# A graph network's two convolution passes: 52 and 52 groups of edges for the two ways of reading, in place of 48 and 56

## The chip, the cores and the metric

The kernel runs on one core of one Trainium2 chip. The metric is the device time of one execution in microseconds (us), with all inputs in HBM at its start and the output there at its end.

## What is computed

The graph has 3125 nodes with 32 features each and 100000 edges, sorted by destination. Four blocks follow each other, each added to its input and normalized by row. Only the second and the third matter here:

```
# block 0: an edge network of four dense layers, averaged per destination (not touched)
# block 1
norm = deg_inv_sqrt[row] * deg_inv_sqrt[col]
x = layernorm(x + segment_sum(x[row] * norm[:, None], col, num_segments=n))
# block 2
h = x * rsqrt(max(deg_out, 1))[:, None]
agg = segment_sum(h[src], dst, num_segments=n) * rsqrt(max(deg_in, 1))[:, None]
x = layernorm(x + relu(agg @ weight + bias))
# block 3: three layers of graph attention (not touched)
```

Both blocks are a convolution of one form: for every edge read one row of a table of 3125 x 32 numbers at the edge's source, and add it up at the edge's destination.

## The kernel before

**The edges.** The sorted edges lie in 832 slots of 128 edges, 8 slots to a group, so 104 groups (`G`). The node numbers are split into 25 windows of 128 nodes (`W`). A slot's destinations lie in one window.

**The table** is written once per pass, to DRAM (`table`, `store_table`, L560) and to SBUF (`tab`). In SBUF each row is also kept as three bf16 parts whose sum is the float32 number (`tabparts`).

**Two ways to handle a group.** The 104 groups are split into two lists, the same in both passes (L55, L56).
- A *plain* group is gathered: GpSimd issues eight indirect DMAs (L396), each of which brings the 128 table rows of one slot into one of four buffers (`rows4`). VectorE makes the one-hot matrix of the destinations for the group's eight slots (L1658). TensorE multiplies (`sum_plain`, L935 to L945, eight matmuls, 128 x 96 each), and VectorE adds four results into the accumulator `acc` (L1617), at windows that it reads from a register load (`found`, L1607).
- A *dense* group is read on TensorE. A stationary matrix `bt` (128 x 1024 for each of four residues, bf16) says which source each edge has modulo 512; a matmul with all of the table picks seven candidates for each edge (`read`, L905 to L920, 24 matmuls for two slots). VectorE masks them by the group of 512 that the source lies in (`gmask`, L1630, and L1638) and reduces them to one (L1645). TensorE then multiplies by the float32 one-hot of the destinations, which SP loads from DRAM (`dhot`, L558), in `sum_dense` (L922 to L933), and VectorE adds the result into `acc` (L1617). This is done in four items of two slots each.

**Who makes `bt`.** In pass 1 it is VectorE, a quarter at each item, one group ahead (`stationary`, L1620, the comparison at L1633). In pass 2 it is ScalarE (`act_stationary`, L736 to L744).

**The order.** `ITEMS` (L59) is a fixed order that TensorE and VectorE both walk: all 192 dense items, with the 56 plain groups spread evenly among them, so three or four dense items lie between two plain groups. TensorE does `read(i)` and then `sum_dense(i - 1)`. Two PSUM banks take the reads and two the sums, so `read(i)` waits for the mask of item i - 2 and `sum_dense(i - 1)` for the reduction of item i - 1. A plain sum waits for its one-hot and for its gathered rows (L937, L938).

**The degrees.** In pass 1 the out-degrees of the nodes are counted as well, in 104 steps spread over the order: ScalarE makes the one-hot (L730, L733), VectorE the other factor (L1670), TensorE does eight small matmuls (`degree`, L947 to L953).

**GpSimd** issues the gathers in order (`pool_convolution`, L380). It waits for the plain sum that frees a buffer (L391) and stays at most `LEAD` = 24 gathers ahead of TensorE's dense reads (L395). **SP** loads for each dense group the numbers of which `bt` is made (`numbers_of`, L538) and the hot matrix, two groups ahead (`sp_convolution`, L548).

Of the kernel before, what the change touches and what calls it, by code (L numbers as in the profile page):

```python
# [27 lines left out]
C = 32  # L28
# [25 lines left out]
GROUPS = -(-W // FOLD)  # L54
DENSE = [g for g in range(G) if 6 * g % 13 >= 7]  # L55
PLAIN = [g for g in range(G) if 6 * g % 13 < 7]  # L56
LEAD = 24
ND, NP, NS = len(DENSE), len(PLAIN), 4 * len(DENSE)
ITEMS = [x for i in range(NS) for x in [("dense", i)] + [("plain", p) for p in range(NP * i // NS, NP * (i + 1) // NS)]]  # L59
BIG = 1e30  # L60
# [14 lines left out]
def build(nc, x, edge_blocks, L0, W_gcn, b_gcn, gat, out):  # L75
    with ExitStack() as ctx:
# [303 lines left out]
        def pool_convolution(pool, pas):  # L380

            if pas == 1:
                pool.wait_ge(small_turned, 1)
            else:
                pool.wait_ge(x_given, 2)
            pool.memset(acc[:, :, 0:3 * C], 0.0).then_inc(acc_zeroed, 1)
            pool.wait_ge(table_stored, 16 * (pas + 1))
            for p_, g in enumerate(PLAIN):
                at = (pas - 1) * NP + p_
                if at >= 4:  # L390
                    pool.wait_ge(plain_summed, at - 3)  # L391
# [142 lines left out]
        def stationary_there(d):  # L534

            return (bt_made, FOLD * (d + 1)) if d < ND else (bt2_made, FOLD * (d - ND + 1))

        def numbers_of(sp, pas, d):  # L538

            at, g = (pas - 1) * ND + d, DENSE[d]  # L540
            if at == 0:
# [6 lines left out]
        def sp_convolution(sp, pas):  # L548

            sp.wait_ge(table_stored, 16 * (pas + 1))  # L550
            for d, g in enumerate(DENSE):
                at = (pas - 1) * ND + d
# [183 lines left out]
        def act_stationary(act, d):  # L736

            b, at = d % 2, d - ND
            act.wait_ge(r_in[b], 16 * (d // 2 + 1))
# [24 lines left out]
        def _(act):  # L764
# [136 lines left out]
        def pe_convolution(pe, pas):  # L901

            base, dbase = (pas - 1) * NP, (pas - 1) * ND

# [55 lines left out]
            counted = 0  # L960
            for n, (kind, i) in enumerate(ITEMS):
                if kind == "dense":
# [3 lines left out]
                else:  # L966
                    sum_plain(i)
                while pas == 1 and counted < G and counted * len(ITEMS) < (n + 1) * G:
                    degree(counted)
                    counted += 1  # L970
            sum_dense(NS - 1)
            if pas == 1:
# [276 lines left out]
        def _(v):  # L1249
# [352 lines left out]
            def gcn(pas):  # L1602

                base, dbase = (pas - 1) * NP, (pas - 1) * ND
                order = [(acc_zeroed, pas)]
# [14 lines left out]
                def stationary(d, k):  # L1620
                    if d >= dbase + ND:
                        return
                    b = d % 2
                    if k == 0:
                        v.wait_ge(r_in[b], 16 * (d // 2 + 1))
                        if d >= 2:
                            v.wait_ge(dense_read, 4 * (d - 1))
                            v.wait_ge(picked_made, 4 * (d - 1))
                        g = DENSE[d - dbase]
                        link(v.tensor_tensor(gmask[:, b, :, :], wide(grp[:, 8 * g:8 * g + 8], GROUPS),  # L1630
# [23 lines left out]
                def plain_one_hot(p_):  # L1654
                    if p_ >= NP:
                        return
                    at, g = base + p_, PLAIN[p_]
                    v.tensor_tensor(hotb[:, at % 2, :, :], wide(dloc[:, 8 * g:8 * g + 8], P), down(ps[:, IOTA, 0:P], 8),  # L1658
# [23 lines left out]
                def run():  # L1682
                    counted = 2
                    for n, (kind, i) in enumerate(ITEMS):
                        if kind == "dense":
                            stationary(dbase + i // 4 + 1, i % 4)
                            pick(i)
                            if i % 4 == 0:
                                places[i // 4 % 2] = found(DENSE[i // 4], C)
                            if i > 0:  # L1690
                                add_dense(i - 1)
                        else:
                            plain_one_hot(i + 1)
                            add_plain(i, found(PLAIN[i], 3 * C))
                        while pas == 1 and counted < G and (counted - 2) * len(ITEMS) < (n + 1) * G:
                            degree_groups(counted)
                            counted += 1
                    add_dense(NS - 1)
                    v.wait_ge(*order[0])
# [347 lines left out]
```

## Time and profile before

| | us |
|---|---|
| median of three runs | 5590.19 |
| lowest and highest of them | 5585.79, 5603.41 |
| the profiled execution | 5609.76 |
| its span | 5608.0 |

Of the span, some 605 us belong to pass 1 of the convolutions (first dense read at 1039.6 us to the last reduction at 1644.4) and 574 us to pass 2 (1664.0 to 2237.6); block 0 is ahead of them and the attention behind. The profile gives for each engine its busy time and its timeline. "issue" as the cause of a wait means that the engine waited for nothing that the profile shows. On GpSimd the time between two gathers is partly work of its own that isn't booked as busy. L943 is a plain sum, L916 a dense read, L931 a dense sum, L951 a degree step; of a float32 sum two matmuls are listed as four.

### The profile page before, as it was taken

What the parts mean: (1) busy time and instruction counts of PE and PEld (TensorE: products, weight loads), DVE (VectorE), ACT (ScalarE), POOL (GpSimd) and SP (SyncE); (2) the same over time, 40 slices, a digit from 0 to 9 for tenths busy, and PEclk for the clock granted to TensorE, in tenths of its full rate; (3) what the DMA queues carried; (4) which work ended last, traced back from release to release, by engine and by line L of the source; (5) the groups of instructions that cost most, each with busy time, mean ns of one, the idle gap of its engine ahead of it and who ended that gap; (6) DMA issues with size and microseconds to landing.
All of it is one profiled execution on the core that took longest, in us unless ns stands there. A gap on an engine that the chain in (4) does not pass through costs nothing.

```text
span 5608.0 us, 137304 instructions
## 1 busy us (share of the span) xinstructions
PE 4951.9 (88%) x47173; PEld 3418.4 (61%) x47173; DVE 3662.6 (65%) x7001; ACT 2121.6 (38%) x3942; POOL 3829.5 (68%) x3980
## 2 busy tenths in 40 slices
PE   4999999789879998599999986999999769999997
PEld 3777777688878888255555552555555535555555
DVE  7566555699987777465666674666666746666667
ACT  2222222466656665233333323333333233333331
POOL 5777777477747776677777716777777177777770
PEclk9999999799989999799999997999999889999998
DMA  5755555233323333344444423444444234444442
GB/s 141 190 169 164 170 164 168 71 96 102 96 78 102 102 102 86 82 128 126 130 127 127 128 71 85 129 128 130 128 126 127 64 95 125 129 130 127 127 126 60
DMA packets 694505, 667.15 MB, mean 119 GB/s; under 512 B 398707, under 2 KB 485242, under 8 KB 693818
## 3 DMA queue, kind: packets, MB, share of 16 engines
q1 hardware_dynamic: 558442, 489.21, 28.8%
q0 software_dynamic: 127424, 164.72, 13.7%
q10 hardware_dynamic: 7952, 4.46, 0.5%
q8 instruction: 383, 6.28, 0.5%
q14 instruction: 304, 2.49, 0.1%
HBM read 568.30 MB, written 89.59 MB: 117 GB/s over the span
## 4 chain that ended last, share of the span: by engine, by line
PE 41%; POOL 26%; issue 19%; DVE 6%; DMA 5%; ACT 2%; DVEq 1%; SPq 0%; POOLq 0%; ACTq 0%
POOL rows L376 16%; PE ps L916 11%; PE ps L1071 10%; POOL rows L363 10%; PE ps L1010 5%; DMA rows<-table,idx 3%; PE ps L1031 3%; PE ps L931 2%; PE ps L1045 2%; PE ps L996 1%; DVE region L1638 1%; ACT region L683 1%; PE ps L1021 1%; DVE acc L1617 1%; PE ps L880 1%
## 5 line engine op out<-in xcount | busy, mean ns | idle before, releaser
L376 POOL DMA_INDIRECT rows<-table,idx x2340 | 2263.2, 967 | 990.5 <-issue 681.6
L1071 PE MATMUL ps<-region,hot 128*128 128x272 f32 x4992 | 1296.2, 404 | 61.8 <-issue 33.5
L683 ACT ACTIVATE region<-ps 128x512 f32<-128x512 f32 x1248 | 678.0, 596 | 1579.1 <-PE ps L1010 1579.1
L1805 DVE TENSOR_TENSOR acc<-acc,ps 128x272 f32 x1248 | 544.9, 437 | 921.2 <-PE ps L1071 812.3
L1071 PEld LDWEIGHTS ps<-region,hot 128*128 128x128 f32 x4992 | 905.1, 191 | 347.0 <-issue 173.2
L916 PE MATMUL ps<-hot,region 128*128 128x192 bf16 (+1 forms) x9216 | 875.4, 253 | 37.8 <-DVEq L1308 20.6
L363 POOL DMA_INDIRECT rows<-table,idx x728 | 703.9, 967 | 243.5 <-issue 220.5
L916 PEld LDWEIGHTS ps<-hot,region 128*128 128x128 bf16 x9216 | 810.4, 101 | 44.9 <-DVEq L1308 20.7
L1780 DVE TENSOR_TENSOR region<-ps,region 128x1056 f32<-128x1056 f32 x582 | 724.9, 1252 | 45.3 <-issue 40.3
L1010 PE MATMUL ps<-xT,wcat 64*128 64x512 f32 x2496 | 710.3, 646 | 9.5 <-ACT region L683 9.2
L396 POOL DMA_INDIRECT rows<-table,idx x448 | 426.6, 952 | 172.2 <-issue 120.2
L396 POOL DMA_INDIRECT region<-table,idx x448 | 426.6, 952 | 137.1 <-issue 119.2
L996 PEld LDWEIGHTS ps<-identb,rows 128*32 128x32 bf16 x7020 | 221.7, 99 | 426.8 <-issue 426.8
L996 PE MATMUL ps<-identb,rows 128*32 128x128 bf16 x7020 | 274.0, 225 | 185.2 <-DMA rows<-table,idx 184.7
L1010 PEld LDWEIGHTS ps<-xT,wcat 64*128 64x128 f32 x2496 | 190.1, 186 | 359.9 <-issue 358.3
L1645 DVE TENSOR_REDUCE region<-region 128x64 f32<-128x448 f32 x384 | 358.1, 933 | 13.2
L730 ACT ACTIVATE region<-iota,region 128x128 bf16<-128x128 f32 x832 | 254.3, 389 | 218.0 <-PE ps L951 215.0
L1031 PE MATMUL ps<-region,attblk 128*32 128x512 f32 x2496 | 315.0, 624 | 0.0
L1638 DVE TENSOR_TENSOR region<-ps,gmask 128x448 f32<-128x448 f32 x384 | 238.0, 620 | 100.3 <-PE ps L916 97.5
L931 PE MATMUL ps<-region 128*128 128x32 f32 x1536 | 220.4, 267 | 67.9 <-issue 59.7
L1497 DVE TENSOR_TENSOR acc<-acc,ps 128x65 f32 x416 | 93.3, 224 | 284.0 <-PE ps L880 180.5
L742 ACT ACTIVATE region<-region,lanes 128x1024 bf16<-128x1024 f16 x192 | 204.8, 1137 | 191.0 <-PE ps L916 191.0
(302 smaller groups left out, 6723.5 us busy)
## 6 DMA issues: line engine op xcount, KB each, us to landing
hot<-hot_dram SPq DMA_DIRECT2D x624, 256.0 KB
turned<-turned_dram SPq DMA_DIRECT2D x624, 128.0 KB
rows<-table,idx POOLq DMA_INDIRECT x3516
hot_dram<-hot SPq DMA_DIRECT2D x104, 512.0 KB
region<-hot_dram SPq DMA_DIRECT2D x96, 512.0 KB
xwin<-table SPq DMA_DIRECT2D x1664, 24.0 KB
region<-r_dram SPq DMA_DIRECT2D x109, 256.0 KB, 5.9
region<-d_dram SPq DMA_DIRECT2D x104, 256.0 KB
```

The lines of the kernel that those rows point to most:

```text
L363: pool.indirect_dma_start(rows[:, g % 3, j, :], None, table, bass.IndirectOffsetOnAxis(ap=idx[:, 8 * g + j:8 * g + j + 1], axis=0)).then_i ...
L376: pool.indirect_dma_start(rows[:, n % 2, j, :], None, table, bass.IndirectOffsetOnAxis(ap=idx[:, s:s + 1], axis=0)).then_inc(rows_in3[n % ...
L396: pool.indirect_dma_start(rows4[at % 4][:, j, :], None, table, bass.IndirectOffsetOnAxis(ap=idx[:, 8 * g + j:8 * g + j + 1], axis=0)).then ...
L683: act.activation(rz[g % 2][:, 2 * t + side, :], ps[:, Z + side, :], ACT.Relu).then_inc(rz_made, 1)
L916: mm = pe.matmul(ps[:, GB + i % 2, 224 * j:224 * j + n], bt[b][:, k, at:at + P], tabparts[:, k::FOLD, (2 + s) * C:(3 + s) * C], start=(k = ...
L996: mm = pe.matmul(ps[q:q + C, XT, j * P:(j + 1) * P], rowparts[(l * G + g) % 2][:, at, 2 * C + s * C:2 * C + (s + 1) * C], identb[:, :], st ...
L1010: pe.matmul(ps[:, Z + side, :], wcat[l][q:q + 64, side, t * P:(t + 1) * P], xT[q:q + 64, g % 2, :], start=True, stop=True).then_inc(z_summ ...
L1031: pe.matmul(ps[at:at + 32, LG, :], attblk[l][:, t, (3 - m) * H:(7 - m) * H], rz[g % 2][:, 2 * t + side, :], start=False, stop=(m == 3 and ...
L1071: mm = pe.matmul(ps[:, sum_bank(k, side, i), 0:PC + H], hot[:, b, 4 * side + 2 * i + j, :], px[b][:, 4 * side + 2 * i + j, :], start=(j == ...
L1645: v.tensor_reduce(found32[:, d % 2, at:at + 2, :], picked[d % 2][:, at:at + 2, :, :].rearrange("p j g c -> p j c g"), AX.X, ALU.add).then_ ...
L1780: v.tensor_tensor(to, at.unsqueeze(3).broadcast_to([P, 4, H, HK]), xs[:, (k // 8) % 2, k % 8, 4 * side:4 * side + 4, :].unsqueeze(2).broad ...
L1805: v.tensor_tensor(at, at, ps[:, sum_bank(k, side, i), 0:PC + H], ALU.add).then_inc(att_added, 1)
```

## The change

The two lists become every odd group (dense) and every even group (plain), 52 and 52, in both passes. The lists, the counts and the order become dictionaries by pass, with offsets (`FIRST_DENSE`, `FIRST_PLAIN`) in place of multiples of the old counts. The new order is: four dense items, one plain group, 52 times. `LEAD` stays at 24. The diff, cut to its core:

```diff
-DENSE = [g for g in range(G) if 6 * g % 13 >= 7]
-PLAIN = [g for g in range(G) if 6 * g % 13 < 7]
+DENSE = {1: [g for g in range(G) if g % 2 == 1], 2: [g for g in range(G) if g % 2 == 1]}
+PLAIN = {pas: [g for g in range(G) if g not in DENSE[pas]] for pas in (1, 2)}
 LEAD = 24
-ND, NP, NS = len(DENSE), len(PLAIN), 4 * len(DENSE)
-ITEMS = [x for i in range(NS) for x in [("dense", i)] + [("plain", p) for p in range(NP * i // NS, NP * (i + 1) // NS)]]
+ND, NP = ({pas: len(of[pas]) for pas in (1, 2)} for of in (DENSE, PLAIN))
+NS = {pas: 4 * ND[pas] for pas in (1, 2)}
+FIRST_DENSE, FIRST_PLAIN = {1: 0, 2: ND[1]}, {1: 0, 2: NP[1]}
+ITEMS = {pas: [x for i in range(NS[pas]) for x in [("dense", i)] + [("plain", p) for p in range(
+    NP[pas] * i // NS[pas], NP[pas] * (i + 1) // NS[pas])]] for pas in (1, 2)}
...
-            for p_, g in enumerate(PLAIN):
-                at = (pas - 1) * NP + p_
+            for p_, g in enumerate(PLAIN[pas]):
+                at = FIRST_PLAIN[pas] + p_
...
-                    read = (8 * p_ + j - LEAD) * NS // (8 * NP)
+                    read = (8 * p_ + j - LEAD) * NS[pas] // (8 * NP[pas])
                     if read > 0:
-                        pool.wait_ge(dense_read, (pas - 1) * NS + read)
+                        pool.wait_ge(dense_read, 4 * FIRST_DENSE[pas] + read)
...
-            for d in range(ND, ND + 2):
+            for d in range(ND[1], ND[1] + 2):
                 act_stationary(act, d)
...
-            for d in range(ND + 2, 2 * ND):
+            for d in range(ND[1] + 2, ND[1] + ND[2]):
                 act_stationary(act, d)
...
-            base, dbase = (pas - 1) * NP, (pas - 1) * ND
+            base, dbase = FIRST_PLAIN[pas], FIRST_DENSE[pas]
...
-            for n, (kind, i) in enumerate(ITEMS):
+            for n, (kind, i) in enumerate(ITEMS[pas]):
```

The rest of it replaces the same names in the same way, on SP, TensorE, ScalarE and VectorE.

## Rows read from the trace of the kernel before

**Rows 1.** Passes 1 and 2: length, busy PE, PEld, DVE, ACT, POOL; clock; DMA.
```profile
1056.91:1640.93 584.02, 522.25 (x6521) 508.43 (x6522) 528.46 (x1169) 366.60 (x907) 420.73 (x439) 0.99 0.34 95
1682.64:2234.11 551.47, 502.04 (x5707) 490.72 (x5707) 430.03 (x886) 366.79 (x230) 414.67 (x439) 0.98 0.35 100
```

**Rows 2.** TensorE's timeline: last plain sum of pass 1, both ends of pass 2.
```profile
1640.93 0.50 PE L943 MATMUL ps<-region 128*128 128x96 bf16 x8
...
1682.64 0.50 PE L943 MATMUL ps<-rows,region 128*128 128x96 bf16 x8
...
2234.11 0.51 PE L943 MATMUL ps<-region 128*128 128x96 bf16 x8
```

**Rows 3.** GpSimd's timeline: last gather of pass 1, first and last of pass 2.
```profile
1610.70 0.95 POOL L396 DMA_INDIRECT region<-table,idx  x1 [0.31 <-PE ps L916]
...
1670.66 0.95 POOL L396 DMA_INDIRECT rows<-table,idx  x1 [8.77 <-DMA table<-hot]
...
2229.95 0.95 POOL L396 DMA_INDIRECT region<-table,idx  x1 [0.30 <-issue]
```

**Rows 4.** TensorE's waits ahead of plain sums, pass 2: us in total, times, longest.
```profile
PE ps L943 <- issue: 21.4, 21, 2.3
...
PE ps L943 <- DVE region L1658: 10.8, 4, 3.0
```

**Rows 5.** VectorE's groups of instructions, pass 1: busy, mean ns, idle before.
```profile
L1645 DVE TENSOR_REDUCE region<-region 128x64 f32<-128x448 f32 x188 | 175.2, 932 | 6.4
...
L1638 DVE TENSOR_TENSOR region<-ps,gmask 128x448 f32<-128x448 f32 x188 | 116.0, 617 | 11.6 <-PE ps L916 11.0
...
L1633 DVE TENSOR_SCALAR region<-region,lanes 128x1024 bf16<-128x1024 f16 x184 | 92.8, 504 | 1.6
...
L1658 DVE TENSOR_TENSOR region<-dloc,ps 128x1024 bf16<-128x1024 f32 x55 | 66.8, 1214 | 0.2 <-issue 0.2
```

**Rows 6.** TensorE's timeline, pass 1, between two plain sums.
```profile
1270.49 0.50 PE L943 MATMUL ps<-rows,region 128*128 128x96 bf16 x8
1270.84 2.22 PE L916 MATMUL ps<-hot,region 128*128 128x224 bf16 x24
...
1273.29 0.35 PE L951 MATMUL ps<-region 128*128 128x25 bf16 x8
...
1282.42 0.50 PE L943 MATMUL ps<-rows,region 128*128 128x96 bf16 x8
```

**Rows 7.** VectorE's timeline, pass 1: one-hots beside the two plain sums of rows 6.
```profile
1271.92 1.21 DVE L1658 TENSOR_TENSOR region<-dloc,ps 128x1024 bf16<-128x1024 f32 x1
...
1283.84 1.21 DVE L1658 TENSOR_TENSOR region<-dloc,ps 128x1024 bf16<-128x1024 f32 x1
```

**Rows 8.** Busy time by engine over seven stretches from plain sum to plain sum.
```profile
1270.49:1282.42 11.93, 10.97 (x138) 10.58 (x138) 10.97 (x25) 7.22 (x19) 8.96 (x10) 1.00 0.35 100
1492.91:1505.06 12.15, 10.97 (x138) 10.58 (x138) 11.08 (x25) 7.21 (x19) 9.39 (x10) 1.00 0.36 100
1568.11:1579.91 11.80, 10.98 (x139) 10.58 (x139) 10.72 (x25) 5.88 (x17) 8.97 (x10) 1.00 0.34 101
1345.32:1356.87 11.55, 11.31 (x137) 10.94 (x138) 10.62 (x25) 6.00 (x18) 8.81 (x10) 0.96 0.35 101
2023.29:2034.16 10.87, 10.37 (x123) 10.17 (x123) 8.82 (x19) 7.98 (x6) 8.22 (x9) 1.00 0.37 108
2162.68:2173.29 10.61, 10.31 (x120) 10.23 (x121) 8.53 (x18) 7.68 (x6) 8.17 (x9) 1.00 0.41 110
1741.98:1752.13 10.15, 10.15 (x120) 10.15 (x121) 7.12 (x16) 6.19 (x5) 7.71 (x9) 1.00 0.38 111
```

**Rows 9.** TensorE's timeline, pass 1: a waiting dense sum, the read behind it.
```profile
1191.76 0.60 PE L931 MATMUL ps<-region 128*128 128x32 f32 x4 [1.67 <-issue]
...
1192.41 3.88 PE L916 MATMUL ps<-hot,region 128*128 128x224 bf16 x24
```

**Rows 10.** GpSimd's gathers of both passes into one buffer pair, min/median/max ns.
```profile
L396 POOL DMA_INDIRECT region<-table,idx x448: 941/947/1196, 1065.7 to 2230.0; - x150
```

More of the change, by code:

```diff
@@ L534, in stationary_there @@
         def stationary_there(d):
-            return (bt_made, FOLD * (d + 1)) if d < ND else (bt2_made, FOLD * (d - ND + 1))
+            return (bt_made, FOLD * (d + 1)) if d < ND[1] else (bt2_made, FOLD * (d - ND[1] + 1))
         def numbers_of(sp, pas, d):
-            at, g = (pas - 1) * ND + d, DENSE[d]
+            at, g = FIRST_DENSE[pas] + d, DENSE[pas][d]
             if at == 0:
@@ L550, in sp_convolution @@
             sp.wait_ge(table_stored, 16 * (pas + 1))
-            for d, g in enumerate(DENSE):
-                at = (pas - 1) * ND + d
+            for d, g in enumerate(DENSE[pas]):
+                at = FIRST_DENSE[pas] + d
                 b = at % 2
@@ L736, in act_stationary @@
         def act_stationary(act, d):
-            b, at = d % 2, d - ND
+            b, at = d % 2, d - ND[1]
             act.wait_ge(r_in[b], 16 * (d // 2 + 1))
@@ L967, in pe_convolution @@
                     sum_plain(i)
-                while pas == 1 and counted < G and counted * len(ITEMS) < (n + 1) * G:
+                while pas == 1 and counted < G and counted * len(ITEMS[pas]) < (n + 1) * G:
                     degree(counted)
                     counted += 1
-            sum_dense(NS - 1)
+            sum_dense(NS[pas] - 1)
             if pas == 1:
@@ L1602, in gcn @@
             def gcn(pas):
-                base, dbase = (pas - 1) * NP, (pas - 1) * ND
+                base, dbase = FIRST_PLAIN[pas], FIRST_DENSE[pas]
                 order = [(acc_zeroed, pas)]
@@ L1620, in stationary @@
                 def stationary(d, k):
-                    if d >= dbase + ND:
+                    if d >= dbase + ND[pas]:
                         return
@@ L1628, in stationary @@
                             v.wait_ge(picked_made, 4 * (d - 1))
-                        g = DENSE[d - dbase]
+                        g = DENSE[pas][d - dbase]
                         link(v.tensor_tensor(gmask[:, b, :, :], wide(grp[:, 8 * g:8 * g + 8], GROUPS),
@@ L1654, in plain_one_hot @@
                 def plain_one_hot(p_):
-                    if p_ >= NP:
+                    if p_ >= NP[pas]:
                         return
-                    at, g = base + p_, PLAIN[p_]
+                    at, g = base + p_, PLAIN[pas][p_]
                     v.tensor_tensor(hotb[:, at % 2, :, :], wide(dloc[:, 8 * g:8 * g + 8], P), down(ps[:, IOTA, 0:P], 8),
@@ L1683, in run @@
                     counted = 2
-                    for n, (kind, i) in enumerate(ITEMS):
+                    for n, (kind, i) in enumerate(ITEMS[pas]):
                         if kind == "dense":
@@ L1688, in run @@
                             if i % 4 == 0:
-                                places[i // 4 % 2] = found(DENSE[i // 4], C)
+                                places[i // 4 % 2] = found(DENSE[pas][i // 4], C)
                             if i > 0:
@@ L1693, in run @@
                             plain_one_hot(i + 1)
-                            add_plain(i, found(PLAIN[i], 3 * C))
-                        while pas == 1 and counted < G and (counted - 2) * len(ITEMS) < (n + 1) * G:
+                            add_plain(i, found(PLAIN[pas][i], 3 * C))
+                        while pas == 1 and counted < G and (counted - 2) * len(ITEMS[pas]) < (n + 1) * G:
                             degree_groups(counted)
                             counted += 1
-                    add_dense(NS - 1)
+                    add_dense(NS[pas] - 1)
                     v.wait_ge(*order[0])
```

## The prediction

> **What bounds the kernel now.** I cut the profile by stage first: only the two convolution passes run differently after the change, so the question is which engine sets the pace in each. A table of busy times over the stretch from the first to the last plain sum of a pass [rows 1] shows three engines nearly full in both: TensorE 522 of 584 us and 502 of 551 us, VectorE 528 and 430 us. GpSimd's 421 and 415 us look like slack, but its timeline corrects that: the 448 gathers of pass 2 start from 1670.66 to 2229.95 us [rows 3], one every 559.29 / 447 = 1.251 us, of which only 0.95 is booked as busy. In pass 2 GpSimd never rests.
>
> So the passes differ. In **pass 1** the last gather starts at 1610.70 us [rows 3] and the last plain sum at 1640.93 us [rows 2]: the gathers are 30 us ahead, and TensorE and VectorE set the end. VectorE has the more work there [rows 1]. In **pass 2** the last gather starts 4.2 us before the last plain sum [rows 2, 3]. The waits name the cost: TensorE waits 21.4 + 10.8 = 32.2 us ahead of plain sums [rows 4]. The longer waits are put down to a one-hot, yet that matrix is made one plain group earlier; what these sums lack is the last gathered row of the group, and I book all 32.2 us as waits for gathers.
>
> **What the change removes and adds, in each pass.** Four plain groups go, four dense ones come, and the order becomes regular: four dense items, one plain group, 52 times over.
> - GpSimd: 32 gathers fewer, 32 x 1.251 = 40.0 us.
> - TensorE: a dense item (24 reads and the sum after it) takes 1273.29 - 1270.84 = 2.45 us, a plain group 1270.84 - 1270.49 = 0.35 us [rows 6]. Together 16 x 2.45 - 4 x 0.35 = +37.8 us.
> - VectorE: 16 times mask and reduction, 0.617 + 0.932, and in pass 1 a quarter of a stationary, 0.504; four one-hots of 1.214 fewer [rows 5]. The additions into the accumulator stay, 16 for 16. That is +28.0 us in pass 1 and +19.9 in pass 2.
> - ScalarE makes the stationaries of pass 2 itself. It is busy 7.98 us in a cycle of 10.87 [rows 8], so a group's matrix is ready before its turn: nothing.
> - SP: four loads of the hot matrix and four of the numbers more per pass. They keep their place, two groups ahead, and run beside gathers that are fewer: nothing. Were a load late, TensorE would stand for as long as it is late, every cycle.
>
> These sums can't simply be taken, since the engines hand items to each other through two PSUM banks. But the new order already stands in the trace. Wherever a plain group ends on a group border and four dense items follow before the next one, the old kernel runs exactly one new cycle; that happens seven times in each pass. So I measure cycles.
>
> **Pass 1.** The cycle from 1270.49 to 1282.42 us takes 11.93 us [rows 6, 8]. TensorE is busy 10.97 and VectorE 10.97 of it [rows 8]; VectorE's rest is mostly a register load at each dense group's start. Does it repeat itself? VectorE starts the one-hot beside the plain sum 1271.92 - 1270.49 = 1.43 us behind TensorE at its start and 1283.84 - 1282.42 = 1.42 at its end [rows 6, 7]: the lag is handed on unchanged, so this is the steady cycle. It also has two degree steps, what each new cycle gets. The seven run from 11.55 to 12.15 us [rows 8], three of them within 0.02 of this one. So 51 x 11.93 = 608.4 us stands against 584.02 [rows 1], **+24.4 us**. The two additions from above agree in kind: VectorE's 28.0, less some of its waits for TensorE of 11.0 us [rows 5].
>
> **Pass 2.** Here the seven are mixed up with gather waits: where TensorE stood before a plain sum, VectorE caught up, and the cycle after it is short, 10.15 us [rows 8], TensorE's bare work (4 x 2.45 + 0.35). Undisturbed it is 10.87 us [rows 8]; three of the seven are within 0.02 of that. The 0.7 us above bare work is TensorE waiting for the first reduction after a plain group: one-hot, four additions and the mask come before it on VectorE. In the new kernel nothing lets VectorE catch up, so 10.87 is the price. A group's gathers take 8 x 1.251 = 10.0 us, less than the cycle, so once ahead they stay ahead. 51 x 10.87 = 554.4 against 551.47 us [rows 1], **+2.9 us**: the 32.2 us of gather waits go, and so does the half-clock work behind them, but 37.8 us of matmuls and a wait for VectorE in every cycle take their place.
>
> Start and tail of each pass keep their order: nothing. **Sum:** 24.4 + 2.9 = +27.3. The profiled execution took 5609.76 us, so its own forecast is 5637. That execution lies 0.35% above the median of the three runs, 5590.19; the difference carries over: 5590.2 + 27.3 = 5617.5, say 5617 us.
>
> **A rule weighed.** A gather is booked with 0.947 us at the median and 1.196 at most, beside all the vector work of both passes [rows 10]. The Trainium skill (SBUF — State Buffer, on the three doors into it) says that while VectorE runs a copy-like instruction in its two-port mode, GpSimd can't write descriptors and the gather waits it out. By it every new comparison would stop the gathers for its length. This trace disagrees on the size.
>
> **The rivals.**
> - *Short cycles hold.* If VectorE's lag settles lower, the cycles are 11.80 and 10.61 us, both seen [rows 8]: 51 x 11.80 - 584.02 = +17.8 and 51 x 10.61 - 551.47 = -10.4, together +7.4, 5598 us. For it: most pass-2 cycles of the kind are under 10.87. Against: each of those follows a wait that goes away. 15%.
> - *Faster: the gathers were the real bound.* The place is the first reduction behind each plain group. If VectorE arrives there in time, as after the old gather waits, pass 2 runs at 10.15, 51 x 10.15 = 517.7, -33.8 us, and pass 1 at its shortest, 11.55 [rows 8], 589.1, +5.0: -28.8, 5561 us. It decides once the two cycles together are below (584.02 + 551.47) / 51 = 22.26 us, where mine are 22.80. Against it: the steady lag of rows 6 and 7, and that the 11.55 had TensorE slow at its start (granted 0.96 [rows 8]). 4%.
> - *The clock.* After a wait of 1.67 us TensorE's next read took 3.88 us in place of 2.2, at the lower of its levels, 1.2 GHz [rows 9]. My cycles are all at 2.4 GHz. If the waits of 0.7 us also bring such drops, they cost about what they cost now, by the granted clock of 0.99 and 0.98 [rows 1]: 0.01 x 584 + 0.02 x 551 = +17, 5634 us. A pass-1 cycle of 12.15 throughout would give as much (+11). 8%.
> - *The gathers become the bound of pass 1.* If each of the four comparisons of a cycle stops GpSimd for its 0.504 us, a group's gathers take 10.0 + 2.0 = 12.0 us, over the 11.93 of the cycle: 51 x 12.0 = 612, +4 on the sum, 5621 us; this is what the rule above makes of it. But the same comparisons run now at gathers 1.251 us apart. 1%.
>
> That the change does not do what it says is excluded by the diff: the lists and their counts give 52 and 52.
>
> **How the numbers follow.** A measurement can tell about 0.3%, 17 us, from no change. The forecast, with 72%, is slower by more; so are the clock and gather rivals, 9% together. The short cycles are within 0.3%, and the faster case is beyond it: slower 0.81, same 0.15, faster 0.04. The range runs from the short cycles, 5598, to the clock's end, 5634; it leaves out the faster case and the outer half of noise.
>
> **What would show it.** Right: plain sums 11.9 us apart in pass 1 and 10.9 in pass 2, to within 0.1; no wait ahead of plain sums in pass 2 after its first cycles; TensorE waiting ahead of the dense sums instead (the line of the 0.7 us), once or twice a cycle; GpSimd's gathers no longer 1.251 us apart throughout but held back by reads; 32 gathers fewer per pass, and everything outside the passes unchanged. Wrong: a pass-2 cycle near 10.15 would say that VectorE catches up by itself; half-clock reads inside the cycles would say that waits of 0.7 us cost clock; a wait for the hot matrix would say that SP's loads are late.

## The result and the profile after

The changed kernel takes **5627.26 us** at the median of five runs (5617.68 to 5638.17), the kernel before 5590.32 us (5585.79 to 5603.41) in five runs beside it. The ratio is **1.0049** with a 95% interval from 1.0033 to 1.0066: slower, by 18 to 37 us. The two medians lie 36.9 us apart, at the upper end of that interval. The profiled execution took 5632.79 us with a span of 5631.0; the one before took 5609.76.

In the code after, everything behind the new lists stands three lines lower: a plain sum is L946, a dense read L919, a dense sum L934, a degree step L954, the addition L1620, the comparison L1636, mask and reduction L1641 and L1648, the one-hot L1661, a gather L399.

First the passes, cut again from the first to the last plain sum (length, busy PE, PEld, DVE, ACT, POOL; clock; DMA), which answers to [rows 1]:

```profile
1060.72:1673.48 612.76, 559.76 (x6939) 539.60 (x6939) 557.01 (x1218) 369.77 (x907) 397.44 (x407) 1.00 0.36 94
1713.89:2267.81 553.92, 528.50 (x6120) 518.44 (x6121) 448.40 (x917) 397.76 (x250) 383.91 (x407) 1.00 0.39 103
```

Pass 1 went from 584.02 to 612.76 us, **+28.7**, pass 2 from 551.47 to 553.92, **+2.5**: +31.2 together. The reader is to see the columns too. VectorE has 28.6 and 18.4 us more work, TensorE 37.5 in pass 1 but only 26.5 in pass 2, where 37.8 were added: most of the missing 11 us are old reads that no longer run at the lower clock (granted 0.98 before, 1.00 now). The 4512 matmuls of the old reads were booked with 427.4 us, the 4896 of the new ones with 453.7; at the new mean the old ones would have taken 9 us less. GpSimd has the 32 gathers fewer.

The span grew by 23.0 only, since the stretches outside the passes together took 8.2 us less: +3.8 ahead of the first plain sum, -1.3 between the passes, -10.7 behind them. Nothing is changed there, and they scatter: in the profiles below, the first plain sum comes between 1043 and 1067 us, and the rest behind pass 2 takes 3361 to 3376 us. So I read every kernel below by its two passes and use the ratios as the check. Where the same pass is profiled again its length repeats to within 3 us: 582.22 to 584.77 for the old pass 1, 553.91 to 555.22 for the new pass 2.

TensorE's waits over the two passes (time in total, times, longest), which answer to [rows 4]; the first row is pass 1, the others are pass 2:

```profile
PE ps L934 <- issue: 52.9, 100, 0.9
...
PE ps L934 <- issue: 25.4, 50, 0.8
PE ps L946 <- issue: 0.7, 1, 0.7
```

The 32.2 us ahead of plain sums in pass 2 have become 0.7. In their place TensorE waits 50 times for 0.5 us ahead of a dense sum (30 times, 16.9 us, before). Such a wait costs 0.7 us: from the read's start to the sum's start it takes 2056.12 - 2053.39 = 2.73 us in place of 2.06, since a sum that needn't wait starts ahead of the booked end of the read. TensorE's and VectorE's timelines over one cycle of pass 2 show the place:

```profile
2050.60 0.50 PE L946 MATMUL ps<-region 128*128 128x96 bf16 x8
2050.94 2.22 PE L919 MATMUL ps<-hot,region 128*128 128x224 bf16 x24
2053.00 0.56 PE L934 MATMUL ps<-region 128*128 128x32 f32 x4
2053.39 2.22 PE L919 MATMUL ps<-hot,region 128*128 128x224 bf16 x24
2056.12 0.60 PE L934 MATMUL ps<-region 128*128 128x32 f32 x4 [0.50 <-issue]
...
2061.46 0.50 PE L946 MATMUL ps<-rows,region 128*128 128x96 bf16 x8
```

```profile
2052.02 1.21 DVE L1661 TENSOR_TENSOR region<-dloc,ps 128x1024 bf16<-128x1024 f32 x1
2053.15 1.11 DVE L1620 TENSOR_TENSOR acc<-acc,ps 128x96 f32 x4
2054.18 0.21 DVE L1633 TENSOR_TENSOR gmask<-region,iota 128x56 f32<-128x56 f32 x1
2054.43 0.62 DVE L1641 TENSOR_TENSOR region<-ps,gmask 128x448 f32<-128x448 f32 x1
2055.08 0.93 DVE L1648 TENSOR_REDUCE region<-region 128x64 f32<-128x448 f32 x1
```

The cycle is 2061.46 - 2050.60 = 10.86 us. The dense sum at 2056.12 needs the reduction that ends at 2056.01; ahead of that VectorE does the one-hot, four additions, the group mask and the mask, in one row without a gap. The one-hot starts 2052.02 - 2050.60 = 1.42 us behind the plain sum, as in [rows 6, 7].

GpSimd's last gather of pass 1 and the first and last of pass 2, which answer to [rows 3]:

```profile
1637.09 0.94 POOL L399 DMA_INDIRECT region<-table,idx  x1 [0.30 <-issue]
...
1702.53 0.95 POOL L399 DMA_INDIRECT rows<-table,idx  x1 [8.07 <-DMA table<-hot]
...
2234.15 0.95 POOL L399 DMA_INDIRECT region<-table,idx  x1 [0.30 <-issue]
```

The gathers end 2267.81 - 2234.15 = 33.7 us ahead of the last plain sum of pass 2, where they were 4.2 ahead. No wait for them is left in this pass but the 0.7 us.

### The profile page after: what moved, and what is told of

Same layout as the page of the kernel before. It is cut to its first block, busy times and chain, and to the rows that moved or that the text cites. A ratio compares the mean times of both kernels' runs of the same rounds, so it can differ in the third digit from the quotient of the medians.

```text
span 5631.0 us, 139144 instructions
## 1 busy us (share of the span) xinstructions
PE 5010.4 (89%) x48005; PEld 3478.4 (62%) x48005; DVE 3712.7 (66%) x7081; ACT 2153.3 (38%) x3962; POOL 3767.1 (67%) x3916
## 4 chain that ended last, share of the span: by engine, by line
PE 46%; POOL 27%; issue 17%; DMA 4%; DVE 3%; ACT 2%; DVEq 0%; SPq 0%; POOLq 0%; ACTq 0%
POOL rows L379 15%; PE ps L919 15%; POOL rows L366 11%; PE ps L1074 11%; PE ps L1013 5%; PE ps L934 3%; PE ps L1034 3%; DMA rows<-table,idx 3%; PE ps L1048 2%; PE ps L999 1%; PE ps L1024 1%; ACT region L686 1%; PE ps L946 1%; PE ps L993 1%; PE ps L874 0%
## 5 line engine op out<-in xcount | busy, mean ns | idle before, releaser
L379 POOL DMA_INDIRECT rows<-table,idx x2340 | 2254.4, 963 | 1019.5 <-issue 687.0
L919 PE MATMUL ps<-hot,region 128*128 128x192 bf16 (+1 forms) x9984 | 932.9, 250 | 20.7 <-DVEq L1311 20.7
L919 PEld LDWEIGHTS ps<-hot,region 128*128 128x128 bf16 x9984 | 865.5, 100 | 22.4 <-DVEq L1311 20.8
L366 POOL DMA_INDIRECT rows<-table,idx x728 | 704.0, 967 | 246.4 <-issue 221.0
L399 POOL DMA_INDIRECT rows<-table,idx x416 | 399.8, 961 | 195.8 <-issue 104.8
L399 POOL DMA_INDIRECT region<-table,idx x416 | 399.7, 961 | 162.3 <-issue 102.4
L1648 DVE TENSOR_REDUCE region<-region 128x64 f32<-128x448 f32 x416 | 388.1, 933 | 14.2
L1641 DVE TENSOR_TENSOR region<-ps,gmask 128x448 f32<-128x448 f32 x416 | 258.1, 621 | 90.6 <-PE ps L919 87.5
L934 PE MATMUL ps<-region 128*128 128x32 f32 x1664 | 240.1, 268 | 85.9 <-issue 80.3
L934 PEld LDWEIGHTS ps<-region 128*128 128x128 f32 x1664 | 219.2, 192 | 116.9 <-issue 110.8
L745 ACT ACTIVATE region<-region,lanes 128x1024 bf16<-128x1024 f16 x208 | 221.9, 1137 | 159.0 <-PE ps L919 159.0
```

The lines of the kernel that those rows point to most:

```text
L366: pool.indirect_dma_start(rows[:, g % 3, j, :], None, table, bass.IndirectOffsetOnAxis(ap=idx[:, 8 * g + j:8 * g + j + 1], axis=0)).then_i ...
L379: pool.indirect_dma_start(rows[:, n % 2, j, :], None, table, bass.IndirectOffsetOnAxis(ap=idx[:, s:s + 1], axis=0)).then_inc(rows_in3[n % ...
L399: pool.indirect_dma_start(rows4[at % 4][:, j, :], None, table, bass.IndirectOffsetOnAxis(ap=idx[:, 8 * g + j:8 * g + j + 1], axis=0)).then ...
L919: mm = pe.matmul(ps[:, GB + i % 2, 224 * j:224 * j + n], bt[b][:, k, at:at + P], tabparts[:, k::FOLD, (2 + s) * C:(3 + s) * C], start=(k = ...
L934: mm = pe.matmul(ps[:, DB[i % 2], 0:C], dhot[b][:, at, :], found32[:, b, at, :], start=(j == 0), stop=(j == 1))
```

## The experiments

What had to be told apart. The first theory (L where a text below uses a letter) is the prediction's: the length of a cycle is set by the chain behind each plain group on VectorE, with the lag that it hands on. Its rivals: VectorE's total of work sets it, whatever the order; the gathers still have a part; and, for the 4.3 us by which pass 1 missed its forecast, gathers that meet a comparison of VectorE (the collision theory, P). The kernel before was run again beside them; its median was 5602.68 us for the first four, 5602.57 for the next four, 5594.05 for the last three. "52" in the table is the new split of a pass, "48" the old; lengths are from first to last plain sum in us.

| run | split, passes 1 and 2 | pass 1 | pass 2 | ratio to before, 95% |
|---|---|---|---|---|
| before | 48, 48 | 584.02 | 551.47 | |
| after | 52, 52 | 612.76 | 553.92 | 1.0049 (1.0033 to 1.0066) |
| e1 | 48, 52 | 584.77 | 555.22 | 1.0006 (0.9991 to 1.0022) |
| e2 | 52, 48 | 611.83 | 550.43 | 1.0041 (1.0024 to 1.0059) |
| e3 one-hot later | 52, 52 | 626.42 | 530.60 | 1.0057 (1.0036 to 1.0078) |
| e4 plain group mid-way | 52, 52 | 601.50 | 542.66 | 1.0027 (1.0014 to 1.0040) |
| e5 one-hot in the first item | 52, 52 | 607.83 | 545.71 | 1.0022 (1.0008 to 1.0036) |
| e6 as e5, pass 2 only | 48, 52 | 582.22 | 545.20 | 0.9981 (0.9971 to 0.9991) |
| e7 LEAD 20 | 52, 52 | 608.16 | 553.98 | one run, 5621.06 us |
| e8 short comparisons | 52, 52 | 584.73 | 553.91 | one run, 5600.12 us |
| e9 one-hot and windows ahead | 52, 52 | 601.53 | 519.87 | 0.9980 (0.9969 to 0.9991) |
| e10 as e9 | 48, 52 | 577.62 | 518.93 | **0.9927** (0.9911 to 0.9944) |
| e11 as e9 | 48, 48 | 578.45 | 550.33 | 0.9990 (0.9978 to 1.0002) |

**The change in one pass alone.**

```diff
-DENSE = {1: [g for g in range(G) if g % 2 == 1], 2: [g for g in range(G) if g % 2 == 1]}
+DENSE = {1: [g for g in range(G) if 6 * g % 13 >= 7], 2: [g for g in range(G) if g % 2 == 1]}
```

> The new split in pass 2 alone; pass 1 keeps 48 and 56 groups. Nothing is left out of the computation. Theory L (the lag theory: VectorE's work behind each plain group, one-hot, four additions, mask, arrives late at the first reduction, so the repeating cycle of four dense items and one plain group costs 12.0 us in pass 1 and 10.87 us in pass 2): pass 1 takes 584 us from first to last plain sum as in the kernel before, pass 2 takes 554 us; +2 to +4 us against the kernel before, about 5593 us. Rival M (the loss is spread over both passes alike, each dense group costs about the same extra in either): half of the +37 us, about 5609 us. Rival S (the short cycles: pass 2 gains once the gather waits go): 10 to 30 us below the kernel before.

e2 has the two lists the other way round.

> The new split in pass 1 alone; pass 2 keeps 48 and 56 groups. Nothing is left out. Theory L: pass 1 takes 613 us from first to last plain sum as in the changed kernel, pass 2 551 us as before; +27 to +31 us against the kernel before, about 5619 us. Rival M: +18 us, about 5609 us. Rival S: as much above the changed kernel as pass 2 gained there.

The loss is pass 1's: 1.0041 with the change in pass 1 alone, 1.0006 with it in pass 2 alone; together 1.0047, against 1.0049 for both. Each pass is as long as in the full change to within 1.3 us (611.83 against 612.76, 555.22 against 553.92), so the passes hardly act on each other.

**The one-hot moved behind the second dense item.** If the chain sets the cycle, pass 2 should fall to TensorE's bare work.

```diff
+                    since, due = -9, 0
...
                             if i > 0:
                                 add_dense(i - 1)
+                            since += 1
+                            if since == 2:
+                                plain_one_hot(due)
                         else:
-                            plain_one_hot(i + 1)
+                            since, due = 0, i + 1
                             add_plain(i, found(PLAIN[pas][i], 3 * C))
```

> The changed kernel, 52 and 52, with VectorE's one-hot for the next plain group made behind the second dense item after a plain group and not beside the plain sum. VectorE does the same instructions. Theory L: the 1.1 us of the one-hot leaves the stretch ahead of the first reduction, TensorE no longer waits there in pass 2, and the cycle there falls from 10.87 to 10.15 to 10.25 us (TensorE's bare work), so pass 2 takes 518 to 523 us and not 554; in pass 1 VectorE is nearly full whatever its order, so the cycle falls only by part of VectorE's wait for TensorE of 0.2 us, to 11.6 to 11.9 us from 12.0: 6 to 20 us. Together 37 to 55 us below the changed kernel. Rival B (the 0.7 us per cycle are TensorE's own, a cost of changing between the kinds of items or of PSUM): both cycles stay, no difference from the changed kernel. Rival T (VectorE's total work sets both passes, not its order): no difference either.

Pass 2 fell by 23.3 us to cycles of 10.38; the 31 to 36 us and the 10.15 to 10.25 of the expectation were not reached. Pass 1 rose by 13.7, to cycles of mostly 12.2 to 12.4: a miss for the chain theory, which had it at 11.6 to 11.9. VectorE's timeline of e3 in pass 1 names what I had not counted:

```profile
1475.93 0.18 DVE L1620 TENSOR_TENSOR acc<-acc,ps 128x32 f32 x1
1476.66 1.12 DVE L1620 TENSOR_TENSOR acc<-acc,ps 128x96 f32 x4 [0.56 <-DVE acc L1620]
1477.70 0.21 DVE L1633 TENSOR_TENSOR gmask<-region,iota 128x56 f32<-128x56 f32 x1
```

Ahead of the four additions VectorE stands 0.56 us. The one-hot used to be issued between; while it ran for 1.21 us, the register load of the windows of those additions passed unseen. The waits of VectorE over pass 1 of e3 say that this happens in every cycle, and that VectorE waits for TensorE only 0.2 + 3.8 us in all 626:

```profile
DVE acc L1620 <- DVE acc L1620: 30.5, 53, 1.0
DVE acc L1620 <- issue: 26.5, 47, 0.6
DVE acc L1620 <- PE ps L934: 3.8, 4, 0.9
DVE region L1641 <- PE ps L919: 0.2, 1, 0.2
```

So in e3 VectorE is full in pass 1, by its two exposed register loads. One edit had taken a piece off the chain and put 0.56 us on the total.

**The plain group in the middle of a dense group.** The chain keeps its one-hot and its hidden register load, but the group mask, made at a dense group's start, leaves it.

```diff
-    NP[pas] * i // NS[pas], NP[pas] * (i + 1) // NS[pas])]] for pas in (1, 2)}
+    NP[pas] * (i + 2) // NS[pas], NP[pas] * (i + 3) // NS[pas]) if p < NP[pas]]] for pas in (1, 2)}
```

> The changed kernel, 52 and 52, with each plain group two dense items earlier: it stands in the middle of a dense group and no longer on the border between two, where VectorE also makes the mask (0.21 us) and reads a register for the windows (0.56 us without work). Theory L: only the mask leaves the stretch ahead of the reduction behind the plain group; the register load comes after that reduction anyway. TensorE's wait in pass 2 falls from 0.7 to about 0.45 us, the cycle from 10.87 to 10.6 us, pass 2 by 12 to 14 us; in pass 1 the cycle stays within 0.2 of 12.0. Together 5 to 20 us below the changed kernel. Rival C (the coincidence with the dense group's border is what costs, register load included): pass 2 falls to 10.2 us per cycle, 35 us. Rival B: nothing changes.

Most cycles fell to 11.72 to 11.75 and 10.60, by 0.2 to 0.3 us; the group mask is booked with 0.21 and takes 0.25 from its start to the next (2054.18 to 2054.43). The same instructions in another order, and both passes are shorter by 11.3 us: order counts, not the sum alone. In pass 1 about half of that probably belongs to another effect, lengthened comparisons (below), of which e4 has few: their mean is 488 ns in place of 517, over some 200 of them. VectorE now waits for reads 3.8 us in all of pass 1, so there it is full, at 11.73 us. Some 7 us were given back ahead of each pass's first plain sum, outside the lengths in the table: it waits 6.9 and 7.3 us, since it now comes before its gathered rows.

**The one-hot in the first dense item, ahead of the register load.**

```diff
                             pick(i)
+                            if due is not None:
+                                plain_one_hot(due)
+                                due = None
                             if i % 4 == 0:
...
-                            plain_one_hot(i + 1)
+                            if True:
+                                due = i + 1
+                            else:
+                                plain_one_hot(i + 1)
```

> The changed kernel, 52 and 52, with the one-hot for the next plain group made in the first dense item after the plain group, between that item's reduction and its register load. The run with the one-hot behind the second item showed that beside the plain sum it had hidden a register load of 0.57 us, which then stood bare. Here it hides the same load of the dense group, so VectorE's total stays as in the changed kernel. Theory L (what counts is how much of VectorE's work stands between a plain sum and the first reduction after it; there it is now 0.57 and not 1.13 us): TensorE's wait in pass 2 falls from 0.7 to 0.1 us, the cycle from 10.87 to 10.25 us, pass 2 to 523 to 526 us; pass 1, where VectorE is full, 11.6 to 11.9 us per cycle, 592 to 607 us. Together 35 to 50 us below the changed kernel. Rival R (an exposed register load costs more than the one-hot that hid it): pass 2 at 10.4 us as with the one-hot behind the second item, pass 1 at 12.2 us. Rival B (the 0.7 us are TensorE's own): no change.

Pass 2's cycle is 10.67, not the 10.25 expected; pass 1's 11.89, at the upper end of what was expected. The additions ahead again wait 0.56 us for their windows, so most of what the one-hot's leaving gave is taken back. e6 does the same in pass 2 alone, with the old list in pass 1.

> A version that might beat both: pass 1 with the old 48 and 56 in the old order, pass 2 with 52 and 52 and the one-hot in the first dense item after the plain group. Nothing is left out. Theory L: pass 1 584 us as before, pass 2 523 to 526 us in place of 551; 25 to 28 us below the kernel before, about 0.5%. Rival R: pass 2 at 530 us, 20 us below the kernel before. Rival M (each dense group costs the same extra in either pass): above the kernel before.

This is the first version that beats the kernel before, by 0.19% and not by the 0.5% expected: pass 2 takes 545.20 us, where 523 to 526 were expected, for the same reason as in e5.

**The collision.** From its sixteenth cycle on, pass 1 of the changed kernel takes 12.05 to 12.08 us in most cycles, in place of the 11.90 to 11.93 before that. Comparisons (VectorE) and gathers (GpSimd) of the changed kernel, first in an early cycle, then in a late one:

```profile
1099.99 0.94 POOL L399 DMA_INDIRECT rows<-table,idx  x1 [0.30 <-issue]
1100.32 0.49 DVE L1636 TENSOR_SCALAR region<-region,lanes 128x1024 bf16<-128x1024 f16 x1
...
1255.30 0.94 POOL L399 DMA_INDIRECT rows<-table,idx  x1 [0.30 <-issue]
1255.86 0.64 DVE L1636 TENSOR_SCALAR region<-region,lanes 128x1024 bf16<-128x1024 f16 x1
...
1258.92 0.48 DVE L1636 TENSOR_SCALAR region<-region,lanes 128x1024 bf16<-128x1024 f16 x1
1259.05 1.17 POOL L399 DMA_INDIRECT rows<-table,idx  x1 [0.30 <-issue]
```

The comparison at 1255.86 is the one in the chain behind the plain group. It starts 0.56 us into a gather and takes 0.15 us more, and the cycle is 0.14 longer. At 1259.05 it is the gather that starts in a comparison and takes 0.23 us more. Not every overlap does this: the comparison at 1100.32 begins 0.33 us into its gather and is not lengthened. The timelines of pass 1, before and after, show where the limits lie. All 95 comparisons that begin 0.49 to 0.69 us into a gather are longer, 0.50 to 0.70 us, and they end 1.18 to 1.20 us behind the gather's start; of the 108 that begin up to 0.45 us into one, none takes more than 0.49. All 88 gathers that begin 0.09 to 0.28 us into a comparison are longer, at least 1.03 us, and they end 1.28 to 1.31 us behind the comparison's start.

The kernel before had such comparisons too, one of them within the cycle that the prediction measured:

```profile
1281.52 0.62 DVE L1633 TENSOR_SCALAR region<-region,lanes 128x1024 bf16<-128x1024 f16 x1
```

That cycle still took 11.93 us, since its comparison is the fourth, behind which VectorE has time: the read that its next mask needs ends at 1282.19, and the mask starts at 1282.23. In the late cycles of the new kernel it is the first that grows, in 31 of the 36 from the sixteenth on. Gathers that run freely drift past the comparisons. In the late cycles they are held back by TensorE, by its plain sums (46.8 us from 1240 on) and its reads (29.4), so they come at the same point of every cycle. To shift them without touching VectorE I set another lead:

```diff
-LEAD = 24
+LEAD = 20
```

> The changed kernel with gathers at most 20 and not 24 ahead of the dense reads. In the changed kernel the cycle of pass 1 is 11.92 us while the gathers still run freely and 12.06 from about the fifteenth cycle on, when they are held back in step with TensorE; from there each cycle has the comparison of its first dense item at 0.64 in place of 0.49 us, beside the end of a gather. Theory P (a gather and a comparison of VectorE delay each other, and held-back gathers meet the same comparison in every cycle): with the gathers at another point of the cycle the late cycles of pass 1 are no longer 12.06: 11.92 if they meet none, up to 12.3 if they meet two or more, and the change comes earlier, at about the eighth cycle; pass 2, without comparisons on VectorE, stays at 10.87. Rival D (the longer late cycles have another cause, such as the loads from DRAM): 11.92 and then 12.06 at the same cycles as in the changed kernel.

VectorE's comparisons over pass 1 (count, busy, mean ns, idle before), in the changed kernel and in e7:

```profile
L1636 DVE TENSOR_SCALAR region<-region,lanes 128x1024 bf16<-128x1024 f16 x200 | 103.5, 517 | 1.8
```

```profile
L1636 DVE TENSOR_SCALAR region<-region,lanes 128x1024 bf16<-128x1024 f16 x200 | 98.9, 494 | 1.8
```

With the mean back at 494 ns, most cycles are 11.90 to 11.93 to the end and pass 1 takes 608.16 us: 4.6 us less for 4.6 us of comparisons. No comparison of a first dense item is longer than 0.5 us in e7, and pass 2 stays at 553.98 us. Comparisons of the fourth item are still lengthened, to 0.53 us and more in 20 cycles, and cost nothing. The gathers are booked with 974 and 975 ns at the mean in e7 and 978 and 979 in the changed kernel; they are lengthened as often, and TensorE has no wait for one in that pass. The Trainium skill (SBUF — State Buffer, on the two sides of the SBUF) calls the port pair of VectorE and GpSimd an exclusive lock: whichever starts first keeps it for its whole instruction. That each delays the other agrees with the rows, if the comparison is of the kind that takes the pair; "for its whole instruction" does not. By it the comparison at 1255.86 would have stood until the gather's end at 1256.24, 0.38 us in place of 0.15, and the one at 1100.32 until 1100.93, where it did not stand at all.

**Less work for VectorE.** From its third dense group on, e8 compares only 128 of 1024 columns of each quarter of the stationary in pass 1. The rest of that matrix is left as it was, so that part of the computation is missing.

```diff
-                        v.tensor_scalar(bt[b][:, k, :], rline[b], lanes[:, k:k + 1], None, ALU.is_equal).then_inc(bt_made, 1)
+                        e = 4 * P if d < 2 else P // 2
+                        v.tensor_scalar(bt[b][:, k, 0:2 * e], rline[b][:, 0:2 * e], lanes[:, k:k + 1], None, ALU.is_equal).then_inc(bt_made, 1)
```

> The changed kernel with VectorE's comparisons of pass 1 cut from 1024 to 128 columns from the third dense group on, so the stationary matrices of pass 1 are wrong there: a part of the computation is left out, to see what VectorE's work is worth. 200 comparisons of 0.5 us become about 0.1 us each. Theory L (VectorE sets pass 1): the cycle falls from 12.0 by 1.2 to 1.5 us, to 10.5 to 10.8 us, where TensorE's bare work with two degree steps (10.55 us) takes over; pass 1 takes 540 to 552 us and not 613. Rival B (TensorE or its hand-over sets pass 1): the cycle stays within 0.3 of 12.0 us. Rival G (the gathers set it): the same.

The cycle fell to 11.46, by 0.45, and not to 10.5 to 10.8. VectorE's timeline of e8 (the comparison is L1637 there, the mask L1642), and then of the changed kernel:

```profile
1272.60 0.25 DVE L1637 TENSOR_SCALAR region<-region,lanes 128x128 bf16<-128x128 f16 x1
1272.76 0.62 DVE L1642 TENSOR_TENSOR region<-ps,gmask 128x448 f32<-128x448 f32 x1
```

```profile
1270.98 0.48 DVE L1636 TENSOR_SCALAR region<-region,lanes 128x1024 bf16<-128x1024 f16 x1
1271.37 0.62 DVE L1641 TENSOR_TENSOR region<-ps,gmask 128x448 f32<-128x448 f32 x1
```

From one start to the next a comparison went from 0.39 to 0.16 us, 0.23 less. Four of them take 0.92 us off VectorE's total. The cycle lost 0.45 (11.91 to 11.46), which is two of them. VectorE's waits for reads grew from 11.3 us to 34.7. So VectorE's total did not set this cycle, the chain did. That the chain crosses two comparisons on its way from the plain group to the waits of TensorE is my reading of the 0.45, not shown apart. The expectation, 10.5 to 10.8, took the whole of VectorE's savings off the cycle and was wrong.

**Both at once: the one-hot moved, and its windows loaded behind it.** The register load goes where e3 has the one-hot, so that it is hidden again, and the additions find their windows in registers. The edit against e3:

```diff
-                    counted = 2
-                    since, due = -9, 0
+                    counted, since, due, held = 2, -9, 0, found(PLAIN[pas][0], 3 * C)
...
                             since += 1
-                            if since == 2:
+                            if since == 2 and due < NP[pas]:
                                 plain_one_hot(due)
+                                held = found(PLAIN[pas][due], 3 * C)
                         else:
                             since, due = 0, i + 1
-                            add_plain(i, found(PLAIN[pas][i], 3 * C))
+                            add_plain(i, held)
```

> The changed kernel, 52 and 52, with the one-hot for the next plain group behind the second dense item (as in the run that moved it there) and the register load of that group's windows behind the one-hot, kept in registers until the plain group's turn. The load is then hidden again, and nothing but four additions and a mask stands between a plain sum and the first reduction. Theory L (the order of VectorE's work behind a plain group sets the cycle of both passes; the split alone does not): pass 2 10.15 to 10.25 us per cycle, 518 to 523 us; pass 1 11.3 to 11.7 us per cycle, 576 to 597 us; 45 to 70 us below the changed kernel, 15 to 35 below the kernel before. Rival T (VectorE's total work sets pass 1): pass 1 at 11.9 us per cycle, since the total is the changed kernel's, and only pass 2 gains. Rival R (loading and keeping the registers ahead costs as much): pass 2 at 10.4, pass 1 at 12.2.

Pass 2 runs at 10.15 us, TensorE's bare work: 519.87 us, of which TensorE is busy 519.87. Pass 1 runs at 11.77 to 11.80 in most cycles, above the 11.3 to 11.7 expected, so as a whole e9 is 10 us below the kernel before and not 15 to 35. VectorE's waits over pass 1 of e9:

```profile
DVE acc L1620 <- issue: 26.9, 48, 0.9
DVE acc L1620 <- PE ps L934: 2.7, 3, 0.9
DVE region L1641 <- PE ps L919: 0.5, 2, 0.4
```

VectorE waits for a read 0.5 us in the whole pass. It is full, as in e4: with one register load left open (0.56 in a cycle, the first row) its total is 11.7 to 11.8 us. The changed kernel's 11.92 stood 0.1 to 0.2 above that. To get pass 1 below, the load of the dense group's windows would have to be hidden as well, beside that of the plain group; no run tries both.

**The same order with each split.** e10 has the old list in pass 1 and the new one in pass 2; e11 the old one in both.

> The same move of one-hot and windows in both passes, with the old 48 and 56 in pass 1 and 52 and 52 in pass 2. Theory L: pass 2 518 to 523 us; pass 1, where gathers allow 56 x 10.0 = 561 us, 565 to 580 us in place of 584; 35 to 50 us below the kernel before. Theory T: pass 1 stays at 584 us, 28 to 33 us below the kernel before.

> The same move in both passes with the old 48 and 56 in both: what the move is worth without the new split. Theory L: in pass 2 the gathers set the time at 56 x 1.251 x 8 = 560 us from first gather to last, so pass 2 stays at 548 to 552 us from first to last plain sum, however little VectorE waits; pass 1 565 to 580 us; 5 to 20 us below the kernel before, and 28 us above the run with the new split in pass 2. Rival N (the new split is worth nothing even without the wait for VectorE): pass 2 at 518 to 523 us here too.

The windows of pass 2 in e10 and in e11, columns as above, and TensorE's waits in e11's:

```profile
1661.91:2180.84 518.93, 518.86 (x6121) 517.89 (x6122) 449.02 (x917) 397.62 (x249) 384.14 (x407) 1.00 0.40 110
```

```profile
1663.89:2214.22 550.33, 502.30 (x5707) 494.06 (x5706) 434.52 (x888) 366.81 (x230) 413.85 (x439) 0.97 0.37 100
```

```profile
PE ps L946 <- issue: 32.9, 17, 3.3
PE ps L946 <- DVE region L1661: 7.7, 7, 1.7
```

e10 takes **5550.01 us** (5543.92 to 5569.68) against 5594.05, the best of all and ahead of both kernels; both its passes are as expected, pass 1 with 577.62 us against 584. In e11 the old split again waits 40.6 us ahead of plain sums, and in each of the seven waits put down to a one-hot that matrix had been ready for 0.2 to 1.0 us: there the gathers set pass 2, and a better order on VectorE changes it by 1.1 us, no more than the same pass differs by between two profiles. As a whole e11 is 3.8 us below the kernel before at the median, within noise, where 5 to 20 were expected. The new split in pass 2 is worth 550.33 - 518.93 = 31.4 us with the new order and -2.5 us without.

## Why the prediction was right

The direction, the size and the mechanism held: 5617 forecast, 5627 measured, inside the range; +27.3 forecast, +18 to +37 by the interval, +36.9 between the medians, +31.2 in the passes. The passes are the test; that the whole time is within 10 us is no more than the stretches outside them scatter by. By its steps:

- **GpSimd's pace bounds pass 2 before.** Right: e11 shows it again with VectorE out of the way. The 32.2 us of waits went to 0.7, and the gathers are now held back by TensorE.
- **The work added.** Right: VectorE +28.6 and +18.4 us against +28.0 and +19.9 (2.6 of the 28.6 are comparisons that grew from 504 to 517 ns), TensorE +37.5 in pass 1 against +37.8. SP's loads and ScalarE's stationaries cost nothing: no wait for either stands among TensorE's, between the first and the last plain sum of a pass.
- **Pass 2 at 10.87.** Right to the hundredth: most cycles take 10.85 to 10.88, the pass 553.92 us against 554.4. The lag of 1.42 us is handed on, only the first cycle is short (10.20), and the rival of short cycles is out.
- **The bound behind it.** Right, and shown by e3, e9 and e10: with the one-hot out of the chain and its windows ahead the cycle is 10.15, and 517.7 was the figure of the prediction's faster rival for just that case (518.93 measured). The change doesn't do it by itself.
- **Pass 1 at 11.93: the term that was mis-sized.** "51 x 11.93 = 608.4" was +24.4 and measured +28.7. The steady cycle was right, as the 11.90 to 11.93 of e7 show. That e7's pass also comes to 608.16 is partly luck: its last cycle is 0.9 us short, which the prediction put at nothing, and four of its cycles take 12.17 to 12.27 (in one of them VectorE stands 0.93 us at a register load in place of 0.56), 1.3 us more together. But the cycle that I measured had gathers that ran freely, and its one lengthened comparison lay where nothing waits for it. In the new kernel the gathers lock to TensorE's rhythm and lengthen the comparison in the chain by 0.15 us in most cycles from the sixteenth on: 4.6 us.
- **The rule weighed.** I looked only at gathers stopped by comparisons, and those cost nothing, as said. The loss came from the other side, a comparison stretched by a gather. The rival named the right pair of instructions, the wrong sufferer, and by chance nearly the size (+4, and 612 us for the pass, where 612.76 were measured). The 0.62 of the comparison at 1281.52 stood in the prediction's own cycle and could have told which side to look at.
- **"VectorE's 28.0, less some of its waits for TensorE" as agreement in kind.** Weak: e8 took twice as much off VectorE's total as the cycle gave back. The chain (11.92) and the total (11.73 in e4, 11.79 in e9) lie so near each other that the sum looked like a confirmation of the cycle. The cycle was the evidence, the sum was not.
- **The clock.** The rival is out: granted 1.00 in both passes, with 100 waits of up to 0.9 us in pass 1. Before it was 0.99 and 0.98.

Left open: why the stretches outside the passes scatter from run to run, by up to 24 us ahead of pass 1 and 15 behind pass 2, why a few cycles of pass 1 hold a longer register load, and whether another lead would also help in e10, which was not tried. The collision rests on one profile of one lead, against the profiles of two kernels that have it (the changed one and e2).

## What to carry to other kernels

When a change makes an irregular order regular, look for the places where the old trace already runs the new order, take a cycle there, and check that what it hands on at its end is what it found at its start; but ask also what runs freely beside it now and will be locked to it then. A wait that is taken away is only the first of those in line: the new split (1.0006 in pass 2 alone) and the new order on VectorE (0.9990) are each worth nothing, and together 0.9927, because in pass 2 each removes one of two bounds that stood within a per cent of each other (551.47 and 553.92 us). Before moving a long instruction, see what it hides on its own engine: here the 1.2 us one-hot covered a register load of 0.56 us.

## What the runs showed of the hardware

- **A comparison and a gather delay each other, but only at certain offsets.** A comparison of 128 x 1024 (0.48 to 0.49 us alone) that began 0.49 to 0.69 us into a gather took up to 0.70 us, 0.64 at an offset of 0.56, and ended 1.18 to 1.20 us behind the gather's start (95 of 95, pass 1 before and after); one that began up to 0.45 us into a gather took at most 0.49 (108 of 108). A gather (0.94 us alone) that began 0.09 to 0.28 us into a comparison took 1.03 us and more, at most 1.215, and ended 1.28 to 1.31 us behind the comparison's start (88 of 88).
- **A register load for a dynamic window costs VectorE 0.54 to 0.57 us** in most cycles where a short instruction of 0.18 us or a reduction precedes it, and nothing where a one-hot of 1.21 us does (e3 against the changed kernel).
- **Waits of TensorE of up to 0.9 us, in every cycle, cost no clock**: 1.00 granted over 612.76 and 553.92 us, while the old order, with waits of up to 3.0 us, had 0.99 and 0.98. In e11, with waits of up to 3.3 us, it was 0.97.
